# A three-layer hybrid kernel (scan, linear attention, routed attention): first stage image by image, one half's convolution as diagonal products, the first stage's end reordered

## The reference

```python
x = x + conv(gn(x))        # layer 0: gn normalises groups of 6 channels over an image
t = tokens(x)
t = t + attn(ln(t))        # layer 1: linear attention with relu features, 12 heads
t = t + ffn(ln(t))         # layer 2: 6 of 12 heads chosen for each image, softmax attention, layer norm

def conv(x):
    xh, z = split(x @ in_proj_w.T)                   # 96 channels each
    xc = silu(depthwise_conv3x3(xh, conv_w) + conv_b)
    xs = [xc by rows, xc by columns, both reversed]  # 4 directions, L = 256 steps
    dts, Bs, Cs = split(x_proj_w @ xs)               # 12, 16, 16 rows for each direction
    dts = softplus(dt_projs_w @ dts + dt_projs_b)
    h[t] = h[t-1] * exp(dts[t] * A) + dts[t] * xs[t] * Bs[t]    # 96 channels x 16 states
    y = sum over directions of (sum over states of h * Cs) + Ds * xs, turned back
    return (layernorm(y) * silu(z)) @ out_proj_w.T
```

## Time and profile before

| what | value |
|---|---|
| median of 3 runs | 478.98 us (478.84 to 479.56) |
| profiled execution | 481.3 us, its span 479.3 us |
| TensorE, VectorE busy | 362.0 us, 356.5 us |
| ScalarE, GpSimd busy | 176.6 us, 199.6 us |
| first and last start of a scan | 52.4 us, 328.1 us |
| mean granted TensorE clock | 0.895 |

### The profile page before, as it was taken

One profiled execution on the slowest core, in us unless ns is written; L12 is line 12 of the kernel. 1 busy time (PEld: TensorE's weight loads), 2 busy tenths in 40 slices (PEclk: granted clock), 3 DMA queues, 4 the chain that ended last, 5 costly groups with the idle time before them and its releaser, 6 DMA issues. The chain is left out here.

```text
span 479.3 us, 5427 instructions
## 1 busy us (share of the span) xinstructions
PE 362.0 (76%) x1641; PEld 207.4 (43%) x1641; DVE 356.5 (74%) x624; ACT 176.6 (37%) x394; POOL 199.6 (42%) x199
## 2 busy tenths in 40 slices
PE   5430565677769785785799999799799999969691
PEld 4220121223323231232456745455676585958450
DVE  6164499999899999999988988987665446344424
ACT  2235345234546353442333433244423401126350
POOL 4405366665758586576356365253111001000001
PEclk9999979877999799777899999999799989597966
DMA  5502221110011211101011110000000000000000
GB/s 126 93 0 55 51 51 34 37 34 22 19 43 38 55 34 37 40 19 45 16 34 33 30 33 0 1 0 1 1 1 17 1 1 16 2 0 1 0 18 16
DMA packets 15742, 12.67 MB, mean 26 GB/s; under 512 B 7280, under 2 KB 11362, under 8 KB 15714
## 3 DMA queue, kind: packets, MB, share of 16 engines
q1 hardware_dynamic: 15713, 12.33, 11.2%
HBM read 2.62 MB, written 0.79 MB: 7 GB/s over the span
## 5 line engine op out<-in xcount | busy, mean ns | idle before, releaser
L544 POOL TENSOR_TENSOR outp<-state,c_rep 128x512 f32<-128x512 f32 x96 | 129.5, 1354 | 94.9 <-PE y_acc L1331 47.7
L971 DVE TENSOR_TENSOR_SCAN state<-decay,inp_bc 128x512 f32<-128x512 f32 x96 | 117.2, 1221 | 6.6 <-DVE inp_bc L962 3.2
L1331 PE MATMUL y_acc<-outp,band 128*96 128x512 f32 x192 | 109.6, 657 | 6.7 <-DVE y_sum L986 3.2
L706 ACT ACTIVATE decay<-step_bc,a_neg 128x510 f32<-128x510 f32 x96 | 64.8, 684 | 55.7 <-PE step_bc L1318 55.5
L1322 PE MATMUL inp_bc<-room_s,spread 96*128 96x512 bf16 x96 | 41.4, 432 | 42.0 <-DVE state L971 41.7
L962 DVE TENSOR_TENSOR inp_bc<-b_rep,inp_bc 128x512 f32<-128x512 f32 x96 | 65.4, 681 | 9.9 <-PE inp_bc L1322 9.8
L488 POOL TENSOR_TENSOR rs<-mv,neg_half 128x2 f32<-128x2 f32 x16 | 11.1, 696 | 121.0 <-DVE mv L1007 121.0
L1318 PE MATMUL step_bc<-room_s,spread 96*128 96x512 bf16 x96 | 40.6, 422 | 17.4 <-DMA room_s<-lo 14.3
L1322 PEld LDWEIGHTS inp_bc<-room_s,spread 96*128 96x128 bf16 x96 | 9.9, 104 | 81.3 <-DVE state L971 77.0
L1331 PEld LDWEIGHTS y_acc<-outp,band 128*96 128x96 f32 x192 | 34.3, 183 | 23.4 <-issue 10.5
L1318 PEld LDWEIGHTS step_bc<-room_s,spread 96*128 96x128 bf16 x96 | 10.4, 108 | 37.7 <-issue 29.0
(11 more groups left out here) (330 smaller groups left out, 639.9 us busy)
## 6 DMA issues: line engine op xcount, KB each, us to landing
b_rep<-bc SPq DMA_DIRECT2D x64, 32.0 KB, 2.0
c_rep<-bc SPq DMA_DIRECT2D x64, 32.0 KB, 2.0
room_s<-hi SPq DMA_DIRECT2D x24, 64.0 KB, 2.0
room_s<-mid SPq DMA_DIRECT2D x24, 64.0 KB, 2.0
room_s<-lo SPq DMA_DIRECT2D x24, 64.0 KB, 2.0
x_tok<-in_x_dram SPq DMA_DIRECT2D x2, 384.0 KB, 3.7
out_dram<-room_g SPq DMA_DIRECT2D x4, 192.0 KB, 2.0
room_a<-in_L_attn_w_qkv_dram SPq DMA_DIRECT2D x1, 432.0 KB, 6.5
```

Source lines behind the costliest of these rows:

```text
L544: g.tensor_tensor(outp[:, u % SLOTS, :], state[:, u % STATE_SLOTS, :], c_rep[:, n % 2, :], ALU.mult).then_inc(S["outp"], 1)
L706: a.activation(decay[:, u % SLOTS, :, 1:L], step_bc[u % 2][:, :].rearrange("p (b l) -> p b l", b=IMG)[:, :, 1:L], ACT.Exp, scale=a_neg[:, ...
L971: v.tensor_tensor_scan(state[:, u % STATE_SLOTS, :], decay[:, u % SLOTS, :, :].rearrange("p b l -> p (b l)"), inp_bc[u % 2][:, :], 0.0, AL ...
L1331: t_.matmul(y_acc[0:DI, :], band[:, at:at + DI], outp[:, u % SLOTS, :], start=(g12 == 0), stop=(g12 == UNITS - 1)).then_inc(S["y_mm"], 1)
```

## The change

- **Statistics, products of the group mean and variance, power and bias** go in two sets of four columns, half 0 first; half 1's set stands behind (`group_stats`, `group_deviations`, `group_rsqrt`, `group_bias`; TensorE's `group_means`, `group_vars`, `turn_input`). The load of out_proj has its own semaphore, so the transposes of in_proj no longer wait for it. Several memsets of VectorE stand later.
- **Half 0's convolution** is nine taps of 256 elements for each image; xh, the gate and the first direction's product are by image too. `d0` is two products of 256 columns.
- **Half 1's convolution** is nine products on TensorE into one bank of the ring: each has a 96 x 96 diagonal matrix of one tap's weights as its stationary operand (`taps`, nine ScalarE operations in the first stage, kept in the rows of tT) and a shifted window of `xpad` as the moving one. Three stand in each of slots 9, 11 and 13; the silu reads the bank and adds the bias in its own operations, in slot 17.
- **End of the first stage**: for the first scan the series, both remainders of hi and of mid are VectorE's, half 1's normalisation comes between softplus and split on ScalarE, z last there, and the gate z is multiplied on VectorE ahead of slot 2. The nine pieces go chunk by chunk (hi, mid, lo of one chunk), each chunk with its own semaphore, awaited at its own unit; the first scan's C copies come behind its first chunk.
- **Preparation of the scans**: the second scan's steps up to the product with the input are three slots later (but none before slot 0, `SECOND_LATER`), those of the split two. From the second scan on `left_of_hi` is on GpSimd, in place, ahead of `left_of_mid`.

The diff, cut to its core:

```diff
+SECOND_LATER = 3
...
+Z_GATED = 2
...
-FRONT_BESIDE = ((1, "xh"), (8, "conv0"), (16, "conv1"), (19, "silu"), (21, "z"))
+FRONT_BESIDE = ((1, "xh"), (9, "conv0"), (11, "conv1"), (13, "conv2"), (17, "silu"), (21, "z"))
...
 def preparing(u, at):
 
     n = (u - at) // UNITS + 1
-    if u == 0 and at < 0:
+    if u == max(0, at + SECOND_LATER - (at > PRE_INP)):
         return 1
-    return n if (u - at) % UNITS == 0 and 1 <= n < SCANS and (at >= 0 or n > 1) else None
...
+        taps = tT[0:DI, :, :].rearrange("p c t -> p (c t)")[:, 0:9 * DI].rearrange("p (i d) -> p i d", i=9)
...
-            sp.dma_start(opw[:], out_proj_w.rearrange("(o p) c -> p o c", p=CK)).then_inc(S["w_in"], 16)
+            sp.dma_start(opw[:], out_proj_w.rearrange("(o p) c -> p o c", p=CK)).then_inc(S["w_op"], 16)
...
-                for part, (src, s) in enumerate(((hi, "hi"), (mid, "mid"), (lo, "lo"))):
-                    sp.wait_ge(S[s], 2 * (n + 1))
-                    for j in range(CHUNKS):
+                for j in range(CHUNKS):
+                    for part, (src, s) in enumerate(((hi, "hi"), (mid, "mid"), (lo, "lo"))):
+                        sp.wait_ge(S[s], 2 * (n + 1))
                         sp.dma_start(stack[CHUNK * part:CHUNK * (part + 1), n % 2, j, :],
-                                     src[CHUNK * j:CHUNK * (j + 1), :, :]).then_inc(S["stack"], 16)
-                if n == 0:
-                    repeat(n, DI + NS, c_rep, "outp", "c_there")
+                                     src[CHUNK * j:CHUNK * (j + 1), :, :]).then_inc(S["stack"][j], 16)
+                    if n == 0 and j == 0:
+                        repeat(n, DI + NS, c_rep, "outp", "c_there")
             for n in range(IMAGES):
...
-            inv_sqrt(grs[:], gve[:], "gn_eps", 1, "gn_rsqrt")
...
+            inv_sqrt(grs[:, 4:8], gve[:, 4:8], "gn_eps", 2, "gn_rsqrt")
...
+            def left_of_hi(n, i):
+
+                pool.wait_ge(S["step"], n + 1)
+                pool.wait_ge(S["hi"], 2 * n + i + 1)
+                g.tensor_tensor(step2[:, i, :], step2[:, i, :], hi[:, i, :], ALU.subtract).then_inc(S["rest"], 1)
...
-            series(0)
-            left_of_mid(0, 0)
-            left_of_mid(0, 1)
             orders(0)
...
                     series(preparing(u, PRE_SERIES))
                 for i in range(2):
+                    if preparing(u, PRE_REST[i]):
+                        left_of_hi(preparing(u, PRE_REST[i]), i)
...
                 if step == "silu":
-                    act.wait_ge(S["conv"], 9 * (h + 1))
-                    if h:
-                        act.wait_ge(S["xs0"], IMG * h)
+                    fetched(act, f"conv_{h}")
+                    act.wait_ge(S["xs0"], IMG * h)
+                    act.wait_ge(S["minus_cb"], 1)
                     for b in range(IMG):
-                        a.activation(sg[:, b * L:(b + 1) * L], conv_out[b], ACT.Exp, scale=-1.0).then_inc(S["conv_e"], 1)
-                    act.wait_ge(S["conv_e"], 4 * h + 2)
...
-            group_normed(0)
+            act.wait_ge(S["gn_bias"], 1)
+            for b in range(IMG):
+                group_normed(0, b)
             act.wait_ge(S["const"], 8)
-            front("xh", 0)
-            front("silu", 0)
-            group_normed(1)
+            for b in range(IMG):
+                evac(f"xh{b}_0", (xpad[:, b, 1:SIDE + 1, 1:SIDE + 1],
+                                  bank(f"xh{b}_0")[0:DI, 0:L].rearrange("p (y x) -> p y x", y=SIDE)))
+            evac("w_fold", (pre_w[:, :, 0:DI], bank("w_fold")[0:DI, 0:DIRS * DI].rearrange("p (k c) -> p k c", k=DIRS)))
+            taken(act, "w_alog")
+            a.activation(a_neg[:], a_log[:], ACT.Exp).then_inc(S["a_exp"], 1)
+            act.wait_ge(S["w_small"], 64)
+            act.wait_ge(S["ones"], 2)
+            for b in range(IMG):
+                gate = sg[:, b * L:(b + 1) * L]
+                act.wait_ge(S["conv"], 9 * (b + 1))
+                a.activation(gate, conv_out[b], ACT.Exp, scale=-1.0).then_inc(S["conv_e"], 1)
+                act.wait_ge(S["conv_e"], 3 * b + 1)
+                a.activation(gate, gate, ACT.Ln, bias=1.0).then_inc(S["conv_e"], 1)
+                act.wait_ge(S["conv_e"], 3 * b + 2)
+                a.activation(gate, gate, ACT.Exp, scale=-1.0).then_inc(S["conv_e"], 1)
+                if b == 0:
+                    for i in range(9):
+                        a.activation(taps[:, i, :], ident[0:DI, 0:DI], ACT.Copy, scale=cw[:, i:i + 1]).then_inc(S["taps"], 1)
 
...
                 act.wait_ge(S["step"] if i else S["sp_max"], n + 1)
                 if n > 0:
-                    act.wait_ge(S["stack"], 16 * 9 * n)
+                    for j in range(CHUNKS):
+                        act.wait_ge(S["stack"][j], 16 * 3 * n)
...
             pre_softplus(0)
-            front("z", 0)
+            act.wait_ge(S["gn_bias"], 2)
+            for b in range(IMG):
+                group_normed(1, b)
             for i in range(2):
                 pre_hi(0, i)
             for i in range(2):
...
+            def group_stats(h):
+
+                for c in range(2):
+                    dve.wait_ge(S["gn_turned"], 2 * h + c + 1)
+                    for b in range(IMG):
+                        v.bn_stats(gst[:, 4 * h + 2 * c + b, :], gn_banks[2 * h + c][0:CK, b * L:(b + 1) * L]).then_inc(S["gn_stats"], 1)
+                dve.wait_ge(S["gn_stats"], 8 * h + 4)
+                for s in range(4 * h, 4 * h + 4):
+                    v.bn_aggr(gmv[:, s, :], gst[:, s, :]).then_inc(S["gn_stats"], 1)
...
+            group_stats(0)
+            group_deviations(0)
+            group_rsqrt(0)
+            group_bias(0)
+            group_stats(1)
...
-                if step in ("conv0", "conv1"):
-                    for i in (range(5) if step == "conv0" else range(5, 9)):
-
-                        window = xpad[:].rearrange("p b y x -> p (b y) x")[:, i // 3:i // 3 + ACC_ROWS, i % 3:i % 3 + SIDE]
-                        sums = acc[:]
-                        if i == 0:
-                            taken(dve, f"xh_{h}")
-                            if h:
-                                dve.wait_ge(S["xs0"], IMG * h)
-                            v.tensor_scalar(sums, window, cw[:, 0:1], cb[:, 0:1], ALU.mult, ALU.add).then_inc(S["conv"], 1)
-                        else:
-                            dve.wait_ge(S["conv"], 9 * h + i)
-                            v.scalar_tensor_tensor(sums, window, cw[:, i:i + 1], sums, ALU.mult, ALU.add).then_inc(S["conv"], 1)
                 if step == "silu":
-                    dve.wait_ge(S["conv"], 9 * (h + 1))
-                    dve.wait_ge(S["conv_e"], 4 * (h + 1))
+                    dve.wait_ge(S["conv_e"], 6 + 4)
+                    fetched(dve, f"conv_{h}")
                     for b in range(IMG):
                         img = slice(b * L, (b + 1) * L)
-                        v.tensor_tensor(xs[:, h, 0, img], conv_out[b], sg[:, img], ALU.mult).then_inc(S["xs0"], 1)
+                        v.scalar_tensor_tensor(xs[:, h, 0, img], bank(f"conv_{h}")[0:DI, img], cb[:, 0:1], sg[:, img], ALU.add,
+                                               ALU.mult).then_inc(freed(f"conv_{h}") if b else S["xs0"], 1)
 
                     v.memset(wsel[h][:], 0.0).then_inc(S["wsel_zero"], 1)
...
+            v.tensor_scalar(cb[:, 1:2], cb[:, 0:1], -1.0, None, ALU.mult).then_inc(S["minus_cb"], 1)
+            for b in range(IMG):
+                taken(dve, f"xh{b}_0")
+                for i in range(9):
+                    window = xpad[:, b, i // 3:i // 3 + SIDE, i % 3:i % 3 + SIDE]
+                    sums = conv_out[b].rearrange("p (y x) -> p y x", y=SIDE)
+                    if i == 0:
+                        v.tensor_scalar(sums, window, cw[:, 0:1], cb[:, 0:1], ALU.mult, ALU.add).then_inc(S["conv"], 1)
+                    else:
+                        dve.wait_ge(S["conv"], 9 * b + i)
+                        v.scalar_tensor_tensor(sums, window, cw[:, i:i + 1], sums, ALU.mult, ALU.add).then_inc(S["conv"], 1)
+            for b in range(IMG):
+                img = slice(b * L, (b + 1) * L)
+                dve.wait_ge(S["conv_e"], 3 * (b + 1))
+                v.tensor_tensor(xs[:, 0, 0, img], conv_out[b], sg[:, img], ALU.mult).then_inc(S["xs0"], 1)
+                if b == 0:
+                    group_deviations(1)
+            group_rsqrt(1)
             dve.wait_ge(S["a_exp"], 1)
             v.tensor_scalar(a_neg[:], a_neg[:], -1.0, None, ALU.mult).then_inc(S["neg_a"], 1)
-            front("silu", 0)
-
-
+            v.memset(wsel[0][:], 0.0).then_inc(S["wsel_zero"], 1)
...
             pre_clip(0)
+            dve.wait_ge(S["sp_exp"], 1)
+            v.tensor_scalar(sps[:], spe[:], -0.5, 1.0, ALU.mult, ALU.add).then_inc(S["sp_t"], 1)
+            dve.wait_ge(S["sp_t"], 1)
+            v.tensor_tensor(sps[:], sps[:], spe[:], ALU.mult).then_inc(S["sp_s"], 1)
             pre_ln(0)
             pre_max(0)
             pre_max_series(0)
```

(50 more changed lines are left out.)

148 lines of the change are left out of this document (75 added, 73 removed).

## The result

| | median of the runs, us | range |
|---|---|---|
| before, same chip | 478.91 | 478.25 to 479.56 |
| changed | 462.12 | 461.67 to 463.01 |

Ratio 0.9652, 95% interval 0.9632 to 0.9672: faster by 16.8 us. Forecast 455.6 (23.4 faster), range 445 to 466. The sign and the range held; the gain fell 6.6 us short. The profiled execution took 463.01 us around a span of 461.3: 0.9 above its median, where that of before stood 2.4 above. So 18.3 us in the traces are 16.8 in the medians.

What follows compares the result with a forecast made beforehand. A chain of dependent steps bounds the first stage, VectorE paces the scans, and VectorE and TensorE share the pace later. 10.3 + 1.8 + 10.3 - 2.5 + 3.5 = 23.4 us faster gives 455.6 us; range 445 to 466.

Steps and rivals of the forecast that it cites:

- split to T0: First stage, from the bf16 split to the first scan's product (T0, 50.51 before): 8.5 us becomes 5.5, gain 3.0.
- first slots, T0 to slot 9, without hi: Second scan gains 3.5 us from earlier c_rep transfers and later softplus; 1.2 and 0.5 come back, net 1.8.
- second half's convolution, slots 9 to 22, without hi: Taps leaving VectorE save 10.3 us; TensorE stalls and later preparation cost 2.5.
- hi remainders: Seven directions' hi remainders move to GpSimd: 8.1 us leaves VectorE, 4.0 and 0.6 are lost, gain 3.5.
- Rival (1): First stage bound elsewhere, by late statistics or weight load or dearer taps: T0 at 44.7, time 460.1 us; chance 0.15.
- rivals (3): TensorE's thirds of the second half's convolution run at half clock, costing 15 us: 468.1 us; chance 0.08.
- (4): Windowed tap products on TensorE stream badly; at 4.5 us each slower than before, 486.8 us; chance 0.04.
- That stalls VectorE by 1.1, 0.9 and 0.3: Between two scans' ends TensorE needs 5.2 us with a third of the convolution's products, so VectorE waits in each third.
- 1.2 comes back: Two second-direction steps, formerly in the stall, now stand in slots 2 and 3 and cost 1.2 us of the 3.5.
- I take 1.58, the same form: Each hi remainder on GpSimd priced at 1.58 us, like the in-place product of the series; the lo remainder takes 1.15.
- 1.0 lost in each of four passes: Before attention, VectorE's clip in slot 9 meets a busy GpSimd: 1.0 us lost a pass, 4.0 in all.
- Rival (2): GpSimd becomes the bound of the first passes; the hi term turns from 3.5 to -1.9: 461.0 us; chance 0.12.

Runs made afterwards that it cites:

- hi_back: Changed kernel with the remainder of hi of the later passes moved back from GpSimd to VectorE; 464.27 us, ratio 0.9677.
- taps_short: Changed kernel with six of the nine TensorE products of the second half's convolution left out, one remaining in each third; 463.79 us, ratio 0.9678.
- silu_split: Changed kernel with ScalarE's three operations of the second half's silu one slot earlier, at 16 instead of 17; 461.24 us, ratio 0.9623.
- pieces_back: Changed kernel with the nine pieces issued part by part again, all awaited before the first unit, c's repeat behind them; 466.73 us, ratio 0.9737.
- second_0: Changed kernel with the second direction's preparation three slots earlier, in slots 0 to 3 as in the kernel before; 464.48 us, ratio 0.9691.
- hi_12: Changed kernel with the hi remainder on GpSimd for the second and third direction only, on VectorE for the five later; 462.23 us, ratio 0.9636.
- taps_back: Changed kernel with the second half's convolution back on VectorE, nine taps at slots 8 and 16, silu at 19; 471.28 us, ratio 0.9816.
- wait_op: Changed kernel with the input weight's transposes waiting for the load of out_proj again; 462.02 us, ratio 0.9631.
- weights_20: Changed kernel with the loading of the second weights' products spread from slot 20 instead of 14; 462.24 us, ratio 0.9639.
- split_hi_12_w20: Changed kernel with the edits of silu_split, hi_12 and weights_20 together; 461.27 us, ratio 0.9628.

## Why the prediction came out as it did

Its terms against the traces. Slots are from the table; "without hi" is the row hi_back. The measured ones add up to 18.4 by rounding.

| term | forecast | measured |
|---|---|---|
| to the first tap | +8.5 | +8.6 |
| taps | -2.1 | -1.9 |
| last tap to split | +0.9 | +1.7 |
| split to T0 | +3.0 | +3.0 |
| first slots, T0 to slot 9, without hi | +1.8 | -0.5 |
| second half's convolution, slots 9 to 22, without hi | +7.8 | +7.6 |
| slots 22 to 95, without hi | 0 | -1.7 |
| hi remainders | +3.5 | +1.6 |
| sum | 23.4 | 18.3 |
| profiled execution against median | 0 | -1.5 |

**Right.** T0 was forecast at 40.2 and came at 39.15; the segments hold to 0.2 but one: last tap to split ran 24.49 to 33.66, 9.2 us in place of 9.9. The clip beside GpSimd's reorderings took 0.82, so 0.4 was lost of the 2.2 that I had charged. Taking 0.51 between the independent 0.38 and the dependent 0.81 of wider rows hit. Rival (1) is refuted. The taps on TensorE: six instructions, three products, took 2.74 in each of the three groups, 0.91 a product, at a granted clock of 1.00; rivals (3) and (4) are refuted. That term was confirmed by undoing it: 7.9 against 7.8. But the match is partly luck. The step "That stalls VectorE by 1.1, 0.9 and 0.3" failed: by taps_short the products' stalls cost nothing net. Against that, the silu, which the forecast left on VectorE at no wait, cost what silu_split gives back, 1.9 by the trace, and the maximum of slot 12 gave the 1.2 that was no part of the forecast.

One reading to set right: the forecast took 1.91 and the input products' 3.70 as half clock, but the profile gives 1.00 for those stretches of the kernel before. That 1.91 is a pair's time at half clock is shown by the changed kernel at 56.05, where the granted clock was 0.50.

**The first slots, term +1.8, came out at -0.5.** The second scan gained 3.5 as forecast, and both causes that were named are confirmed: with the DMA order undone (pieces_back) 1.7 of it goes, with the second direction's steps back in their place (second_0) all of it. The step that failed is "1.2 comes back". It priced the second direction's steps at their own duration. They came back at 2.9 even with 1.2 of hi's relief in them: a maximum of 0.66 took 2.35, TensorE fell to half clock behind it, and the clip of slot 9 waited 1.19. I had read just such a block in the earlier trace rows and applied it to the clip of later passes alone, not to this maximum. Where the steps stand is part of it: in second_0 the same maximum took 1.64, in the kernel before 1.63.

**The hi remainder, +3.5, came out at +1.6** (1.2 by ratios). "I take 1.58, the same form" for a remainder was too high: 14 took 1.15 each, so GpSimd kept up better than feared. The form was not the same, since the remainder's second operand is bf16 as that of lo is, and 1.58 was no price alone: each product of that length began 0.25 to 0.64 behind the start of a VectorE operation that still had 0.45 to run. Where none stood there it took 1.26, as in second_0:
```profile
75.02 1.27 POOL L538 TENSOR_TENSOR sps<-sps,spe 96x512 f32<-96x512 f32 x1
```
The step that failed is "1.0 lost in each of four passes", with full relief beside it. The clips lost 1.5 us in all (6.7 against 5.2), very unevenly: 0.6 in slot 33, 2.1 in slot 45, while that of slot 9 was 1.2 shorter but came behind a wait of 1.2. But the relief was smaller too: 0.8 and 1.0 us at the remainders of the third and fourth pass, 0.6 and less after, in place of 1.16, and ScalarE's casts now wait for GpSimd, the silu behind one of them (88.44). Nearly all of the net gain, 1.9, came in the first two passes; hi_12 puts the other five at nothing. The mark I had set for this ("scans between slots 24 and 48 no closer than before") was met: 56.5 us apart against 55.5. Rival (2), GpSimd as the bound, has its direction but not its -1.9.

**Slots 22 to 95, taken as zero,** lost 1.7 without any edit of theirs. It appears in two steps in hi_back's row, 0.8 between slots 22 and 24, and 0.8 at slot 66. The first belongs to the convolution's move: every kernel but taps_back has it. At slot 22 VectorE's product of the gate waits 2.10 for ScalarE; no run takes that apart.

The second goes with TensorE's clock. In the eight kernels that lose 0.4 to 0.8 us at scan 66 the stretch of half clock before it lasted 1.9 to 3.0 us past the start of scan 64; in the other five, and in the kernel before, it ended 0.4 to 1.5 us behind that start, and they lose 0.15 at most. Two of them from scan 64 on, columns as in the earlier trace rows: hi_back, which loses 0.8, and hi_12, which loses nothing.
```profile
216.50:220.00 3.50, 3.50 (x10) 1.87 (x9) 3.47 (x4) 1.78 (x3) 1.35 (x2) 0.57 0.02 5
215.20:218.70 3.50, 3.50 (x12) 2.12 (x11) 3.45 (x4) 1.78 (x3) 1.93 (x2) 0.78 0.03 5
```
The same is seen behind slot 66, where four of the kernels (taps_back, taps_short, hi_12, wait_op) lose 1.5 to 1.7 by the last scan and the others 0.25 at most. Nearly all of it comes at scans 91 and 92, and these four alone have half clock between scans 88 and 90, where TensorE has no idle time. wait_op and the changed kernel in these two slots:
```profile
291.50:295.20 3.70, 3.70 (x17) 2.67 (x16) 3.63 (x5) 1.35 (x7) 1.26 (x1) 0.55 0.00 0
292.60:296.30 3.70, 3.70 (x30) 2.74 (x29) 3.62 (x4) 1.35 (x7) 1.79 (x2) 1.00 0.00 0
```
In four others (second_0, weights_20, silu_split, split_hi_12_w20) half clock falls in slot 87, where TensorE was busy 2.97 of 4.60 us in the changed kernel, and nothing is lost. Both are read across the traces; no edit moves the clock alone, and why it falls at one slot in one kernel and at another in the next is open.

**Profile against median.** "It stood 2.3 above the median of the runs, 478.98; so 455.6" assumed the same distance for the new kernel; it was 0.9. That is 1.5 of the 6.6.

## What to carry to other kernels

Undoing the parts one at a time gave 1.2, 7.9 and 4.1 us, close to the prices read for the DMA order (5.2) and the convolution (7.8); the largest term, the order of the statistics, was not undone. The errors were mostly in steps that were only moved and so counted at their own duration. Price a moved VectorE operation at what it took beside GpSimd, short and long, not at its best row, and look at what stood beside a GpSimd row before taking it as a price. When a gain depends on which of two engines starts 20 ns earlier (76.23 against 76.25 in second_0), expect other edits to give or take a microsecond or two, and check with several executions before calling a variant better.

## What was not expected of the hardware

- One VectorE tensor_tensor of 96x512 took 0.66, 1.13 or 2.35 us: alone or first, behind the rest of one GpSimd product, behind the rest of two. GpSimd lost about 0.5 (3.02 against 2.48 for its pair) where VectorE had started first.
- Taking two thirds of TensorE's extra products away made the kernel no faster, since their delay had kept two GpSimd instructions apart in slot 12 (1.13 against 2.35 for the maximum).
- fp32 products whose moving operand is a window of 16 in rows of 18 took 0.91 us for 512 columns in a run of three. One alone, in taps_short, took as long as the contiguous pair of y_acc, 1.02:
```profile
75.98 1.02 PE L1460 MATMUL ring<-room_w,tT 96*96 96x512 f32 x2
```
- GpSimd's in-place subtraction of a bf16 tile took 1.15 us (14 of them, 1147 to 1159 ns). Its in-place product of two fp32 tiles of that shape took 1.26 with nothing of VectorE's in its way, 1.44 to 1.72 in the kernel before, where each began while a VectorE operation ran.
- A few microseconds of half clock went with no loss where they fell in slot 87, in which TensorE has idle time, and with 1.5 us where they fell in the next two slots, in which it has none.
